# A Mamba scan pipeline: softplus taken a tile ahead, z first in the shared PSUM bank, dt taken later, and four products with C in one GpSimd instruction instead of two

## The reference, cut to what matters

```
u, z = split(in_proj(seq))                 # 128 inner channels
u  = silu(causal_conv(u, 4 taps) + conv_b)
dt, Bm, Cm = split(x_proj(u))              # rank 4, 16 states, 16 states
dt = softplus(dt_proj(dt) + dt_b)
for every position:                        # h: 128 channels x 16 states
    h = exp(dt * -exp(A_log)) * h + (dt * u) * Bm
    y = sum over states of h * Cm
y  = (y + u * D) * silu(z)
out = out_proj(y)                          # added to the input
```

## Time and profile before

| what | us |
|---|---|
| median of three runs | 2186.56 |
| the profiled execution's own time | 2184.64 |
| its span | 2182.9 |
| layer 0, first `times_b` to last `residual` | 53.9 to 704.0 |
| layer 1, first `times_b` to last `residual` | 1173.8 to 1823.6 |

### The profile page before, as it was taken

The page is one execution under the profiler, slowest core; times in us unless marked ns, Lnnn a source line. Parts: engine busy times, 40 slices in busy tenths (PEclk is TensorE's granted clock), DMA queues, the critical chain, the costliest instruction groups (busy, mean ns, idle before and its releaser), DMA issues. The chain is left out here.

```text
span 2182.9 us, 28861 instructions
## 1 busy us (share of the span) xinstructions
PE 1570.9 (72%) x7776; PEld 1034.5 (47%) x7777; DVE 1358.4 (62%) x1913; ACT 934.6 (43%) x1695; POOL 1171.5 (54%) x980
## 2 busy tenths in 40 slices
PE   6666666666665479999956666666666657299994
PEld 4233333333332379999933333333333324299993
DVE  2877777777777622222245777777777786644443
ACT  5555555555554211111136555555555554011111
POOL 0666666666666044444304666666666673145550
PEclk9777777777776789999978777777777777599996
DMA  4544444444442811111034444444444445111114
GB/s 124 119 110 109 109 109 109 109 109 109 109 109 76 330 35 35 35 36 38 27 114 110 110 110 109 109 109 109 109 109 109 109 109 226 64 42 48 46 46 142
DMA packets 75965, 217.62 MB, mean 100 GB/s; under 512 B 11856, under 2 KB 27408, under 8 KB 72592
## 3 DMA queue, kind: packets, MB, share of 16 engines
q1 hardware_dynamic: 67664, 194.53, 35.1%
q0 software_dynamic: 8256, 22.56, 3.2%
HBM read 178.34 MB, written 38.70 MB: 99 GB/s over the span
## 5 line engine op out<-in xcount | busy, mean ns | idle before, releaser
L671 POOL TENSOR_TENSOR L_hc<-L_h,L_cbq 128x768 f32<-128x768 f32 x384 | 697.2, 1817 | 397.2 <-DVE L_h L588 375.3
L490 ACT ACTIVATE ps<-L_dwq,L_negA 128x384 f32<-128x384 f32 x768 | 429.4, 576 | 247.2 <-DVE L_h L588 236.1
L588 DVE TENSOR_TENSOR_SCAN L_h<-ps,L_h,L_dbu 128x384 f32<-128x384 f32 x288 | 276.3, 1001 | 139.1 <-ACT ps L490 139.1
L588 DVE TENSOR_TENSOR_SCAN L_h<-ps,L_carry,L_dbu 128x384 f32<-128x384 f32 x288 | 276.6, 1002 | 113.6 <-ACT ps L490 113.6
L363 PE MATMUL ps<-L_hc,same 128*32 128x384 f32 x1536 | 189.8, 571 | 183.6 <-POOL L_hc L671 183.5
L575 DVE TENSOR_TENSOR L_dbu<-L_dwq,ps 128x768 f32<-128x768 f32 x288 | 270.3, 939 | 26.2 <-DMA L_dwq<-dw_rows 13.2
L323 PE MATMUL ps<-Xn,L_fold 128*128 (+1 forms) x480 | 155.7, 482 | 82.4 <-DVE L_dw L596 82.4
L323 PEld LDWEIGHTS ps<-Xn,L_fold 128*128 128x128 f32 x480 | 133.0, 299 | 149.1 <-issue 132.5
L1150 DVE COPY Xn<-L_w 128x2048 f32 x86 | 107.8, 1256 | 117.1 <-PE ps L1100 108.4
L679 POOL TENSOR_TENSOR L_dbp<-L_dwq,L_cbq 128x768 f32<-128x768 f32 x96 | 174.2, 1814 | 0.0
L363 PEld LDWEIGHTS ps<-L_hc,same 128*32 128x32 f32 x1536 | 32.1, 115 | 290.0 <-POOL L_hc L671 229.6
(11 more groups left out here) (280 smaller groups left out, 2289.4 us busy)
## 6 DMA issues: line engine op xcount, KB each, us to landing
L_dwq<-dw_rows SPq DMA_DIRECT2D x192, 384.0 KB, 6.2
L_cbq<-cb_rows SPq DMA_DIRECT2D x192, 240.0 KB, 9.8
dw_rows<-L_dw SPq DMA_DIRECT2D x48, 384.0 KB, 2.3
L_w<-in_up SPq DMA_DIRECT2D x16, 1024.0 KB, 12.2
L_w<-in_down SPq DMA_DIRECT2D x8, 1024.0 KB, 26.9
tok_rows<-Xn SPq DMA_DIRECT2D x6, 768.0 KB, 13.1
L0s_got<-results SPq DMA_DIRECT2D x18, 256.0 KB, 2.9
L1s_got<-results SPq DMA_DIRECT2D x18, 256.0 KB, 3.1
```

The costliest lines, as they stand in the source:

```text
L490: nc.scalar.activation(da(r, c), dwq[:, r, c % Q, 0, :], ACT.Exp, scale=negA[:, 0, c:c + 1]).then_inc(sem["da"], 1)
L588: nc.vector.tensor_tensor_scan(h[:, c, :], da(t % 2 if isinstance(t, int) else int(slot is None), c), dbu[:, c % 6, :] if k < Q - 1 else d ...
L671: nc.gpsimd.tensor_tensor(hc[:, 2 * j % 8:2 * j % 8 + 2, :], h[:, 2 * j:2 * j + 2, :], spread(cbq[:, r, k, :]), ALU.mult).then_inc(sem["hc ...
```

## The change

On ScalarE `take_dt` moves from after c = 1 to after c = 2; the two Silus and their table loads from after c = 9 to after c = 7, with z first and u second; the softplus steps and `take_bc` two places forward. `silu_u` has a new wait, for `skip` of the tile that last used the same u buffer. On GpSimd `lost(t + 2)` runs in tile t behind the third product, where `lost(t + 1)` stood at the head, and each `times_c` makes four states (128x1536), four instructions a tile. On TensorE `z_in` goes to the head of the tile; `u_in` is one block, now ahead of `spread_b(t, 2)`; `project_dt` and `project_bc` go ahead of `sum_y(t, 1)`; `project_out(t - 1)` goes behind it. On VectorE `residual` moves from after j = 3 to after j = 6.

```diff
@@ TensorE
             def sum_y(t, r, k):
-                pe.wait_ge(sem["hc"], 8 * t + 2 * k + 2)
+                pe.wait_ge(sem["hc"], Q * t + k + 1)
...
                 if more:
                     add_relu(t + 1)
                     add_log(t + 1)
+                    pe.wait_ge(sem["bc_out"], t + 2)
+                    wait(pe, sem["res"], t - 1)
+                    z_in(t + 1, img1)
                 if not first:
                     sum_y(t - 1, 1 - r, Q - 1)
+                if more == 2:
+                    u_in(t + 2, img2, range(5))
                 spread_b(t, r, 2)
-                if more == 2:
-                    u_in(t + 2, img2, (0, 1))
-                if not first:
-                    if more:
-                        pe.wait_ge(sem["bc_out"], t + 2)
-                    else:
-                        pe.wait_ge(sem["zs"], t + 1)
-                    project_out(t - 1)
                 skip(t, r)
-                if more == 2:
-                    u_in(t + 2, img2, (2, 3, 4))
                 sum_y(t, r, 0)
                 if more:
                     spread_b(t + 1, 1 - r, 0)
-                    wait(pe, sem["bc_out"], t + 2)
-                    wait(pe, sem["res"], t)
-                    z_in(t + 1, img1)
-                sum_y(t, r, 1)
-                if more:
-                    spread_b(t + 1, 1 - r, 1)
                 if more == 2:
                     project_dt(t + 2, r)
                     pe.wait_ge(sem["zs"], t + 2)
                     project_bc(t + 2, r)
+                sum_y(t, r, 1)
+                if not first:
+                    if more == 2:
+                        pe.wait_ge(sem["bc_out"], t + 3)
...
+                    project_out(t - 1)
+                if more:
+                    spread_b(t + 1, 1 - r, 1)
                 sum_y(t, r, 2)
@@ ScalarE
             def silu_u(t, r):
                 act.wait_ge(sem["u_in"], t + 1)
+                wait(act, sem["skip"], t - 1)
...
                     decay(t, r, p, c)
-                    if c == 1 and more:
+                    if c == 2 and more:
                         take_dt(t + 1, [(s_dw_row[r], 16 * (p + 1))])
+                    if c == 7 and more:
+                        nc.scalar.preload_act_table_set(SILU)
+                        silu_z(t + 1, 1 - r)
+                        if more == 2:
+                            silu_u(t + 2, r)
+                        nc.scalar.preload_act_table_set(EXP_LN)
...
-                    if c == 12:
+                    if c == 10:
                         dt_head(t + 2)
-                    if c == 13:
+                    if c == 11:
                         steps(t + 2)[2]()
                         take_bc(t + 2, [(s_cb_row[1 - r], 16 * (p + 1 + r))])
@@ VectorE
-                wait(dve, sem["hc"], 8 * (t - 1) + c // 2 + 1)
+                wait(dve, sem["hc"], Q * (t - 1) + k + 1)
...
-                        if j == 3:
+                        if j == 6:
                             residual(t - 1)
@@ GpSimd
-            def times_c(t, r, p, j):
-                k = j // 2
-                if j == 0:
+            def times_c(t, r, p, k):
+                if k == 0:
                     pool.wait_ge(s_cb[r], 64 * (p + 1))
-                if j % 2 == 0:
-                    wait(pool, sem["y"], Q * t + k - 1)
-                pool.wait_ge(sem["scan"], t * N + 2 * j + 2)
-                nc.gpsimd.tensor_tensor(hc[:, 2 * j % 8:2 * j % 8 + 2, :], h[:, 2 * j:2 * j + 2, :],
-                                        spread(cbq[:, r, k, :]), ALU.mult).then_inc(sem["hc"], 1)
+                wait(pool, sem["y"], Q * t + k - 1)
+                pool.wait_ge(sem["scan"], t * N + Q * k + Q)
+                at = (k % 2) * Q
+                nc.gpsimd.tensor_tensor(hc[:, at:at + Q, :], h[:, Q * k:Q * k + Q, :],
+                                        cbq[:, r, k, :].unsqueeze(1).to_broadcast([P, Q, T]), ALU.mult
+                                        ).then_inc(sem["hc"], 1)
...
             lost(0)
+            lost(1)
...
             def tile(t, r, p, last):
-                if not last:
-                    lost(t + 1)
-                for j in range(N // 2):
-                    times_c(t, r, p, j)
-                    if j in (1, 2):
-                        times_b(t, r, p, j - 1)
+                for k in range(Q):
+                    times_c(t, r, p, k)
+                    if k < 2:
+                        times_b(t, r, p, k)
+                    if k == 2 and not last:
+                        lost(t + 2)
```

More of the change, by code:

```diff
@@ L258, in mamba @@
         sem = {k: new(f"{L}_{k}") for k in
-               ("u_in z_in u zs bc dt_in bc_out abs relu e f g l lost dt dt_out w b dbu dbu_p da scan carry hc y yz out "
+               ("u_in z_in u zs bc dt_in bc_out abs relu e f g l lost dt dt_out w b dbu dbu_p da scan carry hc skip y yz out "
                 "res").split()}
@@ L357, in skip @@
                 wait(pe, sem["yz"], t)
-                nc.tensor.matmul(y_ps, diagD[:], u[:, r, :], start=True, stop=False)
+                nc.tensor.matmul(y_ps, diagD[:], u[:, r, :], start=True, stop=False
+                                 ).then_inc(sem["skip"], 1)
             def sum_y(t, r, k):
-                pe.wait_ge(sem["hc"], 8 * t + 2 * k + 2)
+                pe.wait_ge(sem["hc"], Q * t + k + 1)
                 for g in range(Q):
@@ L432, in tile @@
                     project_bc(t + 2, r)
+                sum_y(t, r, 1)
+                if not first:
+                    if more == 2:
+                        pe.wait_ge(sem["bc_out"], t + 3)
+                    elif more:
+                        pe.wait_ge(sem["zs"], t + 2)
+                    else:
+                        pe.wait_ge(sem["res"], t - 1)
+                    project_out(t - 1)
+                if more:
+                    spread_b(t + 1, 1 - r, 1)
                 sum_y(t, r, 2)
@@ L530, in tile @@
                     decay(t, r, p, c)
-                    if c == 1 and more:
+                    if c == 2 and more:
                         take_dt(t + 1, [(s_dw_row[r], 16 * (p + 1))])
+                    if c == 7 and more:
[4 more added lines that the diff above has]
+                        nc.scalar.preload_act_table_set(EXP_LN)
                     if more != 2:
[L534 to L537, removed]
                         continue
[L539 to L543, removed]
-                    if c == 12:
+                    if c == 10:
                         dt_head(t + 2)
-                    if c == 13:
+                    if c == 11:
                         steps(t + 2)[2]()
                         take_bc(t + 2, [(s_cb_row[1 - r], 16 * (p + 1 + r))])
-                    if c == 14:
+                    if c == 12:
                         steps(t + 2)[3]()
-                    if c == 15:
+                    if c == 13:
                         steps(t + 2)[4]()
@@ L700, in tile @@
             def tile(t, r, p, last):
-                if not last:
-                    lost(t + 1)
-                for j in range(N // 2):
-                    times_c(t, r, p, j)
-                    if j in (1, 2):
-                        times_b(t, r, p, j - 1)
+                for k in range(Q):
[4 more added lines that the diff above has]
+                        lost(t + 2)
             def pair(p):
-                tile(2 * p, 0, p, False)
-                tile(2 * p + 1, 1, p, isinstance(p, int) and p == NT // 2 - 1)
+                last = isinstance(p, int) and p == NT // 2 - 1
+                tile(2 * p, 0, p, last)
+                tile(2 * p + 1, 1, p, last)
             tile_pairs(pool, pair)
```

2 lines of the change are left out of this document (1 added, 1 removed).

## The result

The changed kernel takes 1973.35 us (median of four runs, 1972.7 to 1976.5) against 2186.03 us of the kernel before: ratio 0.903, 95% interval 0.902 to 0.905, 213 us less. The forecast was 2015 us, 172 less, in a range of 1945 to 2095. The direction and the mechanism held; the gain was 41 us larger.

A forecast was written before the change was run, and what follows sets the result against it. Waits between engines bound the kernel; a tile falls from 27.31 to 23.3 us (21.6 plus 35% of 4.7), saving 176 us less 4 at the ends, from 2184.64 to 2012.6, median 2015 us, range 1945 to 2095.

The forecast's parts named there:

- The bound: VectorE has 21.1 us of work a tile; waits between engines, mainly for dt and behind the Silus, make it 27.31.
- The dt wait: VectorE's wait behind take_dt, 2.3 and 0.8 us in alternate tiles: gone at the high clock, 2.5 us at the low.
- The hole: ScalarE's two Silus between table loads, for which VectorE waits 4.0 us a tile: no wait after the change.
- The new wait: Five folds on TensorE ahead of spread_b and skip: VectorE waits nothing at the high clock, 2.2 us at the low.
- 35% low: Share of time at TensorE's low clock, charged on 4.7 us of waits above a 21.6 us tile: 23.3 us.
- the wide product as latency: GpSimd's product of four starts only after a layer's last scan: two more us per layer, 4 in all.
- The clock staying high: Rival: TensorE's clock stays high and VectorE alone bounds, 21.6 us a tile, 1940 us; chance 0.12.
- A clock that stays low: Rival: TensorE's clock stays low in the parts that matter, 26.3 us a tile, 2147 us; chance 0.08.
- a drain behind the table load: Rival: ScalarE drains after each table load, hole 2.8 us longer, 26.1 us a tile, 2138 us; chance 0.02.
- a costly product of four: Rival: GpSimd's product of four costs more than twice that of two and bounds the kernel, 2336 us; chance 0.03.
- the waits only change places: Rival: dt still late behind sum_y(2), u behind the folds; period near 27.3, 2187 us, give or take 20; chance 0.05.

The follow-up runs named there:

- the dt part alone: Kernel before, with only lost(t + 2) in tile t behind the sixth pair of products and take_dt after c = 2: 2148.45 us, ratio 0.983.
- with pairs: Changed kernel with the products with C two to an instruction again instead of four: 2032.73 us, ratio 0.930.
- the ten small products: Changed kernel with products in pairs, plus ten small unread matmuls on TensorE ahead of the folds: 1960.27 us, ratio 0.896.
- the twelfth run: Changed kernel with products in pairs, spread_b(t, 2) ahead of the folds and ten small products ahead of both: 1953.33 us, ratio 0.893.

## Why the prediction was right, and where it was off

**The bound.** Right. 21.1 us of work per tile on VectorE and two waits of ScalarE; the waits went from 253.9 to 14.6 us, "under 80" in the prediction.

**The dt wait.** Right in kind. With `lost` late again 136 us come back; with the dt part alone 38 us go. What the prediction named as late next, `sum_y(2)`, is indeed the link: ScalarE still waits 102.7 us for dt, and hides it. Its time was off. The prediction put dt at 2.3 us into the tile at the high clock; the trace has the scan at 303.74 and `take_dt` at 305.00, after 1.3 us. So there was 1 us more of slack. Most of it is a slip in the working: the prediction counts the next tile from 21.1, the bare work, though its tile is 21.6 long, and it starts `sum_y(2)` at 20.4 though its product is done at 20.1. By its own numbers dt is there at 1.5 us, or 4.3 at the low clock, where the wait is then 1.7 us and not 2.5. The rest is the product of four, 3.44 us for the 3.6 taken.

**The hole.** Right: 3.7 us from the first load to the decay, as laid out (7.5 to 11.2 in the tile), and a wait of 0.26 us instead of 4.0. Its place matters more than its inputs: after c = 9 it costs 92 us.

**The new wait.** Right, and the best part: nothing at the high clock, 1.1 to 2.1 us in seven tiles where the folds were low (2.2 worked out). It also named what to cure.

**The step that failed** is the term "35% low: 21.6 + 0.35 x 4.7 = 23.3 us a tile". The measured tile is 22.28, and (23.3 - 22.3) x 44 = 45 us covers the miss of 41. The low share itself was 26%, by the stage's 0.87. But the price was wrong. The term charges 0.35 x 4.7 x 44 = 72 us of waits; the scans waited 14.6 us for decays and `times_b` 10.3 for `spread_b`, 25 in all. Some 12 us of the miss are the slip above (0.35 x 0.8 x 44). The rest is that a share of the stage was multiplied by a cost that belongs to two places of the tile.

The first is the chain of dt. In about half of the tiles at least one softplus addition took over 1.3 us, yet dt has the slack to hide most of that: VectorE waited over half a us in seven tiles, 1.9 us at most, and in six of them `sum_y(2)` and all three additions had been low. One of the six, from the timeline:

```profile
214.30 1.65 PE L344 MATMUL ps<-L_sp_r,ident 128*128 128x384 f32 x2
...
217.02 1.49 PE L350 MATMUL ps<-L_sp_a,ident 128*128 128x384 f32 x2
...
219.63 1.02 DVE L587 TENSOR_TENSOR_SCAN L_h<-ps,L_h,L_dbu 128x384 f32<-128x384 f32 x1 [1.44 <-ACT ps L492]
```

The second is the folds. In this kernel they mostly run at the high clock (368 ns on average, 523 with pairs): `sum_y(3)`, held back by the wide product, leaves a pause of 1.7 or 2.1 us ahead of them in most tiles. The 3.45 us above followed one of 2.77, and with pairs it is 3.3 or 4.4. Other low stretches fall on `sum_y(1)` and `project_out`, which have slack.

**GpSimd.** The prediction priced the wide product as latency (4 us at the two ends) and gave it nothing else. On the kernel before it costs 83 us; inside the change it is worth 59 us against pairs, by the clock at the folds, as the ten small products show. It is latency there too: with pairs ScalarE waits 5.8 us for dt instead of 102.7, and once the folds' clock is cured the pairs are 13 us faster. None of these figures was in the prediction.

**The rivals.** The clock staying high (1940 us) was the nearest; the twelfth run, with a stage clock of 0.94, comes within 14 us of it. A clock that stays low, a drain behind the table load and a costly product of four did not occur. That the waits only change places is half true of the dt part alone.

**What stays open.** The pairs of tiles in the changed kernel vary between 43.8 and 46.5 us by the two waits above: the longest has 1.14 us for `spread_b` (at 201.33) and the 1.44 us for dt shown. Why the clock is low in some tiles and not in others is open: in the run with pairs and small products, pauses of 1.97 us ahead of the folds were followed by folds of 1.89 us in some tiles and of 3.2 to 3.5 in others. How far the small products could be cut was not tried.

## What to carry to other kernels

Where an engine's clock depends on what it did just before, ask not for its mean but for its level at the instruction that someone waits for, and price the low clock at that place alone. A longer instruction on an engine with room to spare can be a loss (latency in a chain) or a gain (it closes a pause ahead of another engine's critical work); take the chain apart before crediting the instruction. When a removed wait gives less than it was long, look for an instruction elsewhere that has become longer. When a slow switch has to be made, put it where the consumer has most work queued, and nothing slow behind it.

## What the runs showed of the hardware

- Ten small matmuls ahead of the folds made them faster, 3.56 to 1.89 us, and the kernel 72 us faster, with TensorE's instructions in the stage up from 1589 to 2029.
- The same trick at another place lifted the mean clock just as much (0.74 to 0.86) and gave 7.6 us. The stage's mean clock alone did not tell the time.
- GpSimd's multiply costs 994, 1817 and 3438 ns at 384, 768 and 1536 columns: 2.1 us per thousand columns and under 0.2 us fixed, no penalty for the wider form.
- A VectorE copy of 128x16 between tiles in SBUF took 0.17 or 0.18 us in every run but one. In the run with the dt part alone it started while a GpSimd product was under way and took 1.29 to 1.47 us, 22 times of 22, until that product's end. Why it is held is not shown.
- Behind a table load of 1.28 us the next activation starts within 0.02 us (311.27 to 312.56), in the new order too. The Trainium skill's drain of 1.38 us (ScalarE: Activation LUTs, What ACT_TABLE_LOAD costs) is not in this trace.
